# Scores of the second tile of queries and of the third and first tile issued one behind the other

## What is computed

```python
x = x + 0.5 * ffn(layernorm(x))
x = x + attention(layernorm(x))
x = x + 0.5 * ffn(layernorm(x))

# attention: 16 heads of 64, causal
qkv = x @ W_qkv
score = einsum('bihd,bjhd->bijh', q, k) / 64 ** 0.5      # masked above the diagonal
out = einsum('bijh,bjhd->bihd', softmax(score), v) @ W_out

# ffn: 8 experts, 4 of them chosen for a row, and a shared one; 341 hidden units each
out = swiglu(x, Ws1, Ws2, Ws3) + sum_e weight_e * swiglu(x, W1[e], W2[e], W3[e])
```

## Time and profile before

| | |
|---|---|
| median of 3 runs | 685.54 us (685.2 to 688.0) |
| span of the profiled execution | 683.0 us |
| around the span (median less span) | 2.5 us |
| PE busy | 646.1 us, 95% |
| DVE busy | 609.6 us, 89% |
| ACT busy | 572.8 us, 84% |
| POOL busy | 495.7 us, 73% |

### The profile page before, as it was taken

How to read it: one execution, slowest core, us unless ns; L and a number is a source line. 1 busy time by engine, 2 the same in 40 slices (tenths; PEclk the granted TensorE clock), 3 DMA queues, 4 the chain that set the end, 5 groups by cost and what they waited for, 6 DMA issues and landing times.

```text
span 683.0 us, 20985 instructions
## 1 busy us (share of the span) xinstructions
PE 646.1 (95%) x7846; PEld 414.1 (61%) x7846; DVE 609.6 (89%) x1701; ACT 572.8 (84%) x1110; POOL 495.7 (73%) x589
## 2 busy tenths in 40 slices
PE   5798989999999998999899999999999999999997
PEld 3465755465567565666566566665666567666665
DVE  4899799999998999899889999989999888789887
ACT  6789977898999888899978999997999997565654
POOL 3244775688899687788967889895789898566555
PEclk9999999999999999999999999999999999999999
DMA  7800000278799366588844788683678797100000
GB/s 205 258 1 1 1 2 1 54 111 148 120 129 154 57 104 120 100 140 123 145 75 79 114 140 141 125 137 56 102 125 134 144 144 110 33 1 18 17 2 16
DMA packets 226489, 62.97 MB, mean 92 GB/s; under 512 B 213202, under 2 KB 225620, under 8 KB 226388
## 3 DMA queue, kind: packets, MB, share of 16 engines
q1 hardware_dynamic: 226388, 61.64, 52.4%
HBM read 7.87 MB, written 1.05 MB: 13 GB/s over the span
## 4 chain that ended last, share of the span: by engine, by line
PE 45%; DVE 23%; ACT 16%; issue 9%; POOL 5%; DMA 1%; SPq 0%; ACTq 0%; DVEq 0%; POOLq 0%
PE bank L1068 13%; PE bank L1070 12%; PE bank L1069 12%; ACT probs L1424 6%; DVE probs L1710 4%; DVE glu L1619 3%; DVE xs L1649 3%; ACT glu L1386 3%; PE bank L1238 3%; DVE glu L1624 3%; POOL paired L1035 2%; ACT gluh L1407 2%; PE bank L1201 2%; POOL glul L1031 1%; ACT paired L1432 1%
## 5 line engine op out<-in xcount | busy, mean ns | idle before, releaser
L1031 POOL TENSOR_TENSOR glul<-glu,gluh 128x512 f16<-128x512 f32 x191 | 221.3, 1161 | 98.4 <-ACT gluh L1407 97.9
L1035 POOL TENSOR_TENSOR paired<-probs,paired 128x512 f16<-128x512 f32 x160 | 185.4, 1161 | 27.4 <-ACT paired L1432 24.5
L1386 ACT ACTIVATE glu<-bank,tanh_scale 128x512 f32<-128x512 f32 x167 | 113.3, 678 | 49.1 <-PE bank L1070 48.5
L1619 DVE SCALAR_TENSOR_TENSOR glu<-glu,bank 128x512 f32<-128x512 f32 x167 | 113.7, 681 | 24.8 <-ACT glu L1386 24.4
L1424 ACT ACTIVATE probs<-probs,exp_bias 128x128 f32<-128x128 f32 (+3 forms) x256 | 131.6, 551 | 3.6 <-POOL exp_bias L1043 3.5
L1710 DVE CUSTOM_DVE_ANT_0 probs<-bank,causal,score_scale 128x128 f32<-128x128 f32 (+3 forms) x256 | 128.0, 545 | 6.2 <-POOL paired L1035 5.0
L1068 PE MATMUL bank<-w3h,gluh 128*128 128x128 f16 x708 | 127.4, 220 | 5.9 <-POOL glul L1031 4.9
L1070 PE MATMUL bank<-w3h,glul 128*128 128x128 f16 x708 | 127.2, 220 | 0.0
L1069 PE MATMUL bank<-w3l,gluh 128*128 128x128 f16 x708 | 127.2, 220 | 0.0
L1407 ACT ACTIVATE gluh<-glu 128x512 f16<-128x512 f32 x191 | 118.5, 621 | 2.0 <-DVE glu L1624 2.0
L1624 DVE SCALAR_TENSOR_TENSOR glu<-glu,bank 128x512 f32<-128x512 f32 x167 | 114.7, 687 | 5.8
(11 more groups left out here) (236 smaller groups left out, 1619.8 us busy)
## 6 DMA issues: line engine op xcount, KB each, us to landing
pT<-paired SPq DMA_TRANSPOSE x160, 3.2
attention_raw<-in_L_attn_W_qkv SPq DMA_DIRECT2D x6, 256.0 KB, 5.3
xs<-in_L_attn_inputs SPq DMA_DIRECT2D x4, 256.0 KB, 4.7
vh<-in_L_ffn_W SPq DMA_DIRECT2D x6, 128.0 KB
pT<-in_L_ffn_W SPq DMA_DIRECT2D x6, 128.0 KB
out<-xs SPq DMA_DIRECT2D x3, 256.0 KB, 2.5
raw_more<-in_L_ffn_W SPq DMA_DIRECT2D x4, 128.0 KB
attention_raw<-in_L_attn_W_out SPq DMA_DIRECT2D x2, 256.0 KB, 6.4
```

Source lines behind the costliest of these rows:

```text
L1031: pool.tensor_tensor(glul[pair][:, :], g[:, :], gluh[pair][:, :], ALU.subtract).then_inc(glu_low)
L1035: pool.tensor_tensor(paired[n % PAIRED][:, 1, :], probs[n % PROBS][:, :], paired[n % PAIRED][:, 0, :], ALU.subtract).then_inc(probs_low)
L1386: act.activation(g[:, :], psum[b1.bank][:, :], ACT.Tanh, scale=tanh_scale[:, j:j + 1]).then_inc(tanh_made)
L1619: v.scalar_tensor_tensor(g[:, :], g[:, :], 1.0, psum[b1.bank][:, :], ALU.add, ALU.mult).then_inc(drained[b1.bank])
```

## The change

The planner gets a second dictionary that says at which unit scores are issued. `SCORED` still says which tiles belong together and when they are softened. At unit 2 the planner now adds two steps `scores`, that of tile 1 and behind it that of tiles 2 and 0, and none at unit 3. The two banks of tiles 2 and 0 are filled before the step of feed forward and the `weigh` of unit 2 and softened at unit 3 as before.

```diff
@@ -71,6 +71,9 @@
 SCORED = {0: ([3], [0, 1]), 2: ([1], [2]), 3: ([2, 0], [3, 4])}
+
+
+SCORED_AT = {0: [0], 2: [2, 3]}
@@ -513,9 +516,9 @@
         def scores(n):
             gp, u = b * PAIRS + n // NU, n % NU
-            if 0 <= n < last and u in SCORED:
+            for of_unit in SCORED_AT.get(u, []) if 0 <= n < last else []:
                 uses = [self.bank() for _ in range(2)]
-                tiles, units = SCORED[u]
+                tiles, units = SCORED[of_unit]
                 self.add("scores", gp=gp, tiles=tiles, uses=uses, qk_ready=self.qk_ready[gp])
                 self.scored_last[gp] = uses
                 for k, of in enumerate(units):
```

## The result

The changed kernel takes 694.26 us (median of 4 runs, 693.42 to 696.47), the kernel before 686.64 in runs beside it. The ratio is 1.0117, 95% interval 1.0090 to 1.0143: slower by 8.0 us (by this ratio; the two medians are 7.6 apart). I had said 689.8, so slower, with the right sign and a size that is too small by nearly half (4.3 against 8.0).

A forecast was written before the change was run, and what follows sets the result against it. Beside attention PE (97%), DVE (93%) and ACT (92%) were all near their limit, none alone setting the pace. 3.9 + 1.6 + 1.1 - 2.3 = +4.3 us on the 685.54 median gave 689.8 us, range 679.8 to 697.

The forecast's parts named there:

- What is removed: One leaving and one entering of the 64-row form per pair, 0.19 us; 5.7 us at most, 2.3 counted as saved.
- Pairs with a hidden tile: In 18 pairs moved scores delay the hidden tile and its tanh; charged 3.9 us plus 1.6 us in 480:565.
- the pair that I replayed: Pair at 303.33: scores stall 0.90 us for a bank, hidden tile 1.57 late, ACT idles 0.79 us.
- the ten pairs of the full stretches: Hidden-tile pairs in four stretches where ACT is 98 to 99% busy: 6.1 us, charged 3.9.
- a first pair of a stretch counts whole, later ones 40%: Weighting of hidden-tile delays within a stretch, as later pairs' banks are already late; turns 6.1 us into 3.9.
- The other five: Hidden-tile pairs where ACT has room, as at 239.07, where it waited 0.70 us anyway; nothing charged.
- the second stall: PE stalls at the unit behind for a bank awaiting softening; up to half a microsecond more per pair, upper end only.
- The three of 480:565: Hidden-tile pairs where ACT is nearly as full: 0.67, 0.47 and 1.92 us, charged 1.6 us.
- Pairs with a weighing alone: In six of 12 the weighing no longer hides in a bank wait, 0.38 us each; three charged, 1.1 us.
- rival 1: PE paces everywhere and stalls spend only spare lead, so the saving arrives whole: 679.8 us, some 682 with half; chance 0.23.
- rival 2: A wait changes its place; PE's saving is spent on uncovered weighings: 685.5 us, within 2 us; chance 0.29.
- rival 3: New stalls bring three more 3.4 us stretches at the 1.2 GHz clock, +5.1 us on top: 694.9 us; chance 0.05.

The follow-up runs named there:

- put_back: Changed kernel with one small matmul of 128 rows and 8 columns between the two score groups, restoring the change of rows; 1.0153 against the kernel before.
- only_bare: Against the kernel before, score steps issued behind one another only in the pairs with nothing but a weighing between them; 1.0002.
- weigh_first: Against the kernel before, score steps behind one another only in pairs without a hidden tile, with the weighing ahead of both; 1.0003.
- only_hidden: Against the kernel before, score steps issued behind one another only in the 18 pairs with a hidden tile between them; 1.0126.
- banks_first: TensorE's order with moved scores behind both products of the hidden tile, but their two banks taken before the tile's; 1.0163 against the kernel before.
- banks_only: Kernel before with the moved scores' two banks taken at unit 2, but the scores issued at their old place, a unit later; 1.0205.
- row_changes: Kernel before with one small matmul between the 384-column and the 128-column scores, adding a change of rows in each of 32 pairs; 1.0047.
- behind_hidden: Changed kernel, but where a hidden tile follows, moved scores go behind both its products and ahead of its down product; 1.0017 against the kernel before.

## Why the prediction was right, and where its size was off

The sum was +4.3 us. Beside attention the trace has +8.7, and +10.3 without what the clock gave back. So the forecast is short by more than its total shows, and part of its nearness is luck.

*What is removed* (0.19 us in 30 pairs, of which I counted 12, 2.3 us). Right in size as far as it is shown, by put_back (2.5 by the ratios, 2.2 by the traces). No tanh is earlier by it in only_bare or weigh_first, so it is not felt in the pairs without a hidden tile; it is felt in some of the others.

*Pairs with a hidden tile.* The mechanism held to the hundredth in the pair that I replayed, and by the experiments the loss is in these pairs. For the ten pairs of the full stretches I had 3.9 us, and the tanhs behind the moved scores are 3.8 later. This is luck in part. The rule "a first pair of a stretch counts whole, later ones 40%" does not hold: the first of 290:330 lost 0.50 of the 0.97 worked out for it, its second the whole 0.79, its third 0.57 of 1.08. The working was exact in three pairs (0.39, 0.79, 0.79) and right with 0 in the pair at 134.98, and too high in the other six. In the pair of 429.28 it let the tile wait for its own bank, the one freed by L1726. On the chip that bank was free, and the tile followed the scores at once (437.31 and 437.37 for the last scores, 437.53 for the tile, with no idle time), so that it lost 0.52 and not 0.95.

*What was put at nothing* is the mis-sized term. "The other five lie where ACT has room; nothing is charged": their tanhs came 3.75 us later and 1.7 of it stayed. By PE's yardstick the five have only 0.65, but that has the clock's 1.6 in it. And the second stall, which I had left to the upper end, reaches tanhs: 8.8 us of PE's waits, 1.00 us at the tanh of 440.67 alone. What it costs in all was not parted from the rest. The three of 480:565, forecast 1.6, have 1.30, 0 and 1.22 us at their tanhs, and part of it is won back.

*Pairs with a weighing alone*, charged 1.1. Right: three tanhs of only_bare are later by 0.36 to 0.37 each, and the changed kernel has the same three steps, which only_hidden has not. One of 0.28 comes on top. That PE's yardstick shows these pairs 1.7 us shorter is lead won back from the pairs ahead of them. In only_hidden, where nothing is moved in them, they are shorter by 2.8.

*Work or banks.* In the replay I had both: the stall for L1619's bank (0.90) and the 0.77 us of scores. Both delay the tile by hand. At the tanh of 305.41 the banks alone give 0.66 us in banks_first and banks_only, of the 0.79 of the changed kernel. With the tile's banks two places back, its first product waits for the L1624 of 305.15 even with nothing ahead of it. In other pairs the banks alone give less or nothing (the tanh of 385.26 is 0.78 later in the changed kernel, and on time in both). So both parts count, in shares that differ by pair.

*The rivals.* The whole saving (rival 1) fell: added PE time is about half felt in row_changes. A wait that only changes its place (rival 2) fell with the measured loss. The clock (rival 3) fell: beside attention the granted clock stays at the 2.4 GHz level after the change (1.00 in 120:575), where before one stall of 2.03 us stood ahead of a stretch at 1.2 GHz; it moved the time the other way, by 1.6 us. The Trainium skill's warning on cycling through banks ("TensorE: Matmul & The Clock Gate", section "A second HAM failure mode: psum-queue depth-cycling") is not borne out by the changed kernel, where PE's waits at banks rose and no such stretch followed. The other versions do not settle it. In behind_hidden a stall of 1.87 us ends at 276.19, and the stretch from 276.4 is at 0.50; in the changed kernel a stall of 1.87 us ends at 276.26, and the clock stays at 1.00:

```profile
276.19 0.41 PE L1089 MATMUL bank<-xnT,wqkvh 128*128 128x512 f16 x1 [1.87 <-DVE xs L1675]
276.40:279.80 3.40, 3.40 (x18) 2.01 (x17) 3.26 (x9) 2.91 (x6) 2.88 (x4) 0.50 0.42 81
```

```profile
276.26 0.39 PE L1071 MATMUL bank<-xnT,wqkvh 128*128 128x512 f16 x1 [1.87 <-DVE xs L1652]
276.30:279.70 3.40, 3.40 (x34) 2.26 (x35) 3.26 (x9) 3.05 (x7) 3.01 (x4) 1.00 0.25 48
```

## What to carry to other kernels

Where banks go round in one queue, the order in which the planner takes them is an order of waiting in its own right: a product that moves ahead takes its banks ahead too, and whoever comes behind it gets those that are freed last. So ask of each moved step whose bank it takes, and try the same instructions with the banks dealt otherwise, which adds no instruction. And put what another full engine is waiting for (here the tanh's product) first, together with its bank: behind that one product the same scores cost a fifth. And before a difference of a few us between two versions is explained by their order, compare the clock of the same stretches, also where the versions do the same work.

## What was not expected of the hardware

Leaving and entering the form with 64 rows costs 0.10 and 0.09 us in the trace, but 32 such pairs of changes, 7.0 us of TensorE with the small matmul, made the kernel only 3.2 us longer, with TensorE 97% busy beside attention. Here a busy share of 97% is not a bound: four engines that wait for each other share it.

A single stretch of 3.4 us at the 1.2 GHz level is worth 1.64 us in the time beside attention: where it is missing, the tanhs from 277.96 on are earlier by that. This is more than one of the terms of the prediction, and nothing in the edit says whether such a stretch comes.
